# Row maxima of the attention scores in two waves per step, with jobs placed anew and the values behind them

## The reference

```python
# L0: attention over 1024 positions with 32 latent channels, then a second one over 128 concepts
th, ph, g = conv1x1(x, w_theta), conv1x1(x, w_phi), conv1x1(x, w_g)
sa_out = gamma_sa * conv1x1(softmax(th^T ph) applied to g, w_o) + x
out = gamma_moca * conv1x1(attention(conv1x1(sa_out, w_theta), concepts), w_o) + sa_out
# L1: class scores, norms, a small gate network; prob * gate is projected back and added to x
# L2: per image: group norm (32 groups), qkv, 8 heads of 32 channels, attention over 1024 positions
weight = softmax((q * scale)^T (k * scale));  h = w_proj @ (weight @ v) + b_proj;  x = x + h
# L3: group norm, qkv, attention of the 8 heads of one position among each other, projection, + x
```

## Time and profile before

| | |
|---|---|
| median of 3 runs | 1922.93 us (1922.35 to 1927.69) |
| the profiled execution | 1920.26 us, span 1918.5 us |
| busy share PE / DVE / ACT / POOL | 89% / 72% / 41% / 71% |
| L0's two windows with the work of L0 and L1 between | 53.5 to 235 us |
| rest of L0 and L1, first image prepared | 235 to 369 us |
| sixteen windows of L2 | 369.4 to 1469 us |
| L3 | 1469 to 1918.5 us |

### The profile page before, as it was taken

How to read it: one execution, slowest core, us unless ns; L and a number is a source line. 1 busy time by engine, 2 the same in 40 slices (tenths; PEclk the granted TensorE clock), 3 DMA queues, 4 the chain that set the end, 5 groups by cost and what they waited for, 6 DMA issues and landing times.

```text
span 1918.5 us, 37187 instructions
## 1 busy us (share of the span) xinstructions
PE 1702.5 (89%) x15160; PEld 773.6 (40%) x15160; DVE 1374.5 (72%) x2153; ACT 787.1 (41%) x1546; POOL 1357.7 (71%) x581
## 2 busy tenths in 40 slices
PE   5897765799999999999999999999997678889974
PEld 2332222344344444344344344444442345555541
DVE  5677567887777877767867877777771158878875
ACT  0352401155455555455455455455555233333320
POOL 0573600088788887887888878878789059989996
PEclk8898887799999999999999999999998889999986
DMA  5000030220001001001001010010010211222211
GB/s 189 1 2 1 2 129 0 84 77 23 2 2 67 2 2 67 2 9 60 2 24 45 2 59 11 1 67 2 2 45 1 89 29 55 88 77 75 74 51 47
DMA packets 48432, 75.11 MB, mean 39 GB/s; under 512 B 30804, under 2 KB 31110, under 8 KB 48262
## 3 DMA queue, kind: packets, MB, share of 16 engines
q1 hardware_dynamic: 38758, 72.15, 10.6%
q10 hardware_dynamic: 9504, 0.59, 0.3%
HBM read 44.87 MB, written 25.17 MB: 37 GB/s over the span
## 4 chain that ended last, share of the span: by engine, by line
PE 77%; DVE 13%; issue 3%; ACT 2%; DMA 2%; POOL 1%; SPq 1%; POOLq 0%; DVEq 0%; ACTq 0%
PE AV L652 14%; DVE MX L1292 7%; PE S L626 6%; PE RB L895 6%; PE S L688 4%; PE S L603 3%; PE AV L908 3%; PE RB L626 3%; PE RB L944 3%; PE S L638 2%; PE RB L603 2%; PE S L630 2%; PE S L678 2%; PE RB L688 2%; PE S L634 2%
## 5 line engine op out<-in xcount | busy, mean ns | idle before, releaser
L1201 POOL TENSOR_TENSOR ACC<-ACC,PR 128x1024 f32<-128x1024 f32 x360 | 840.9, 2373 | 34.4 <-ACT PR L1034 34.4
L1034 ACT ACTIVATE PR<-S 128x512 f32<-128x512 f32 x667 | 358.6, 603 | 373.1 <-PE S L638 242.9
L1292 DVE TENSOR_REDUCE MX<-S 128x1 f32<-128x512 f32 x646 | 409.4, 681 | 124.2 <-PE RB L603 60.5
L1201 POOL TENSOR_TENSOR ACC<-PR 128x1024 f32<-128x1024 f32 x72 | 168.9, 2368 | 343.0 <-ACT PR L1034 131.6
L652 PE MATMUL AV<-PR,VT 128*32 128x512 f32 x2304 | 312.9, 616 | 3.8 <-ACT PR L1034 3.3
L1292 DVE TENSOR_REDUCE MX<-RB 128x1 f32<-128x512 f32 x336 | 218.5, 681 | 73.8 <-PE S L603 57.0
L1034 ACT ACTIVATE PR<-RB 128x512 f32<-128x512 f32 x328 | 183.7, 604 | 168.9 <-PE S L638 63.4
L626 PE MATMUL S<-HI 32*128 32x512 f32 x667 | 195.6, 493 | 6.2 <-DVE NMR L1305 2.5
L1227 POOL TENSOR_TENSOR PR<-WO,WRK 128x1792 f32<-128x1792 f32 x32 | 155.6, 4883 | 27.9 <-DMA WO<-WO 12.9
L1227 POOL TENSOR_TENSOR PR<-WO,VT 128x1792 f32<-128x1792 f32 x32 | 155.0, 4867 | 10.3 <-DMA WO<-WO 8.3
L603 PE MATMUL S<-HI 32*128 32x512 f32 x646 | 156.2, 507 | 3.4 <-ACT PR L1034 2.8
(11 more groups left out here) (357 smaller groups left out, 3250.9 us busy)
## 6 DMA issues: line engine op xcount, KB each, us to landing
X<-out_y SPq DMA_DIRECT2D x24, 1024.0 KB, 5.0
out_y<-X SPq DMA_DIRECT2D x16, 1024.0 KB, 4.9
X<-in_x SPq DMA_DIRECT2D x8, 1024.0 KB, 8.5
OHU<-out_y SPq DMA_DIRECT2D x8, 512.0 KB, 4.4
X<-out_y SPq DMA_DIRECT2D x8, 512.0 KB, 4.1
out_y<-X SPq DMA_DIRECT2D x8, 512.0 KB, 3.1
out_y<-OHU SPq DMA_DIRECT2D x8, 512.0 KB, 3.1
WO<-WO SPq DMA_DIRECT2D x128, 16.0 KB, 1.9
```

The costliest lines, as they stand in the source:

```text
L1034: nc.scalar.activation(exps(s, pair)[:, HALF * one:HALF * one + HALF], RING[ring.place()], ACT.Exp, scale=1.0 if i is None else float(D) * ...
L1201: nc.gpsimd.tensor_tensor(ACC[:, pair, :], so_far, exps(s, pair), ALU.add).then_inc(pool_used, 1)
L1292: nc.vector.tensor_reduce(out=MX[:, h, t, keys:keys + 1], in_=bank(), op=ALU.max, axis=AX.X).then_inc(ring_free, 1)
```

## The change

1. **Waves.** A tile of maxima (four heads) becomes two waves of two heads, and the keys' first half is done for all tiles before the second. Each of the eight steps of a half carries two waves: `max` is the first job of the step and `late` the last.
2. **Order on PE.** Values no longer follow the scores: the order is scores, first wave, job, second wave, values. Where a step has no job with a bank, the second wave goes behind the values. The last step of each half does the values of the step before and its own, then the flip; the first step of a half has no values.
3. **Banks.** `Ring.begin` lays down the banks of a step ahead, in the order in which they are expected to come free, in place of strict turns.
4. **Jobs** move: q/k products from steps 1, 2, 3 and 11 (or 15) to 2, 4, 10 and 11 (or 12); value products are two of four key tiles (were four of two), at 0 or 3 and at 8; `post` from 4, 6, 12, 15 to 3, 5, 12, 15; statistics, `gn` up to two steps later. `QK_ORDER` is k, q, k, q.
5. **Waits.** `scores` waits for the flip only before its last round. The semaphore `stage_ready` goes; PE waits for the count of drained banks instead. ACT copies `AV` (`keep_values`) ahead of the exponents of the first step of a half.

```diff
     def begin(self, jobs, single):
+        held = []
+        def take():
+            if not self.free:
+                self.free.append(held.pop(0))
+            self.step.append(self.free.pop(0))
+            return self.step[-1]
+        for _ in range(H):
+            held.append(take())
+        for job in jobs:
+            for n in range(places(job, single)):
+                slot = take()
+                held.insert(2 * n + 1 if job[0] == "max" else len(held), slot)
+        self.free += held
...
-QK_ORDER = ((1, 0), (1, 1), (0, 0), (0, 1))
+QK_ORDER = ((1, 0), (0, 0), (1, 1), (0, 1))
...
-            for n, tile in enumerate(maxima(1 - half)):
-                jobs[first + (n if n <= SUM_AT else n - 1)].append(tile)
-            jobs[first + MT - 1] += [("negate", 1 - half), ("flip", 1 - half)]
+            waves = maxima(1 - half)
+            for step in range(first, first + MT):
+                jobs[step].append(waves.pop(0))
+                late[step] = [("late",) + waves.pop(0)[1:]]
+            jobs[step] += late[step] + [("negate", 1 - half)]
+            late[step] = [("flip", 1 - half)]
...
-        for step, job in zip((1, 2, 3, MT + (3 if post or gn or single else 7)), QK_ORDER):
+        for step, job in zip((1, 2, 3, MT + 3) if single else (2, 4, MT + 2, MT + (3 if gn else 4)), QK_ORDER):
-        parts = (6, MT + 1) if single else (7, MT + 1, MT + 1, MT + 2) if gn else (4, 6, 7, MT + 2)
+        for n, step in enumerate((6, MT + 1) if single else (0 if gn else 3, MT)):
...
-        for step, job in zip((4, 6, MT + 4, MT + 7), ((0, 0), (1, 0), (0, 1), (1, 1))):
+        for step, job in zip((3, 5, MT + 4, MT + 7), ((0, 0), (1, 0), (0, 1), (1, 1))):
...
-        jobs[first + 1].append(("stats", 1, ahead))
-        jobs[first + 2].append(("gn", 0, ahead))
+        jobs[first + (2 if ahead == 2 else 1)].append(("stats", 1, ahead))
+        jobs[first + (4 if ahead == 2 else 3)].append(("gn", 0, ahead))
...
@@ window of PE @@
+                    ring.begin(jobs[s], i is None)
                     scores(u, par, s)
-                    if s:
-                        values(u, par, s - 1)
-                    for job in jobs[s]:
+                    last = s % MT == MT - 1
+                    idle = all(places(job, i is None) == 0 or job[0] in ("max", "late") for job in jobs[s])
+                    behind = [job for job in jobs[s] if job[0] == "flip" or job[0] == "late" and idle and not last]
+                    for job in jobs[s][:len(jobs[s]) - len(behind)] + [("values",)] + behind:
+                        if job[0] == "values":
+                            if s % MT:
+                                values(u, par, s - 1)
+                            if last:
+                                values(u, par, s)
```

More of the change, by code:

```diff
@@ L137, in window_jobs @@
         jobs[first].append(("stats", 0, ahead))
-        jobs[first + 1].append(("stats", 1, ahead))
-        jobs[first + 2].append(("gn", 0, ahead))
+        jobs[first + (2 if ahead == 2 else 1)].append(("stats", 1, ahead))
+        jobs[first + (4 if ahead == 2 else 3)].append(("gn", 0, ahead))
     if gn:
-        jobs[MT + 4].append(("gn", 1, 1))
-    return jobs
+        jobs[MT + 5].append(("gn", 1, 1))
+    for step, stage in side:
+        jobs[step].append(stage)
+    return [job + waves for job, waves in zip(jobs, late)]
 AFTER = [("reread", 0), ("encode", 0), ("concepts", 0), ("softmax", 0), ("encode", 1), ("turn", 0), ("mix", 0),
@@ L154 @@
 AFTER_AT = (3, 3, 4, 5, 5, 6, 7, 7, 8, 9, 10, 10, 11, 12, 13, 13, 14, 15)
-START = [("v", 0)] + maxima(0)[:4] + [("v", 1)] + maxima(0)[4:] + [("negate", 0), ("flip", 0), ("weights",)]
+START = [("v", 0)] + maxima(0)[:8] + [("v", 1)] + maxima(0)[8:] + [("negate", 0), ("flip", 0), ("weights",)]
 def after_jobs():
-    jobs = window_jobs(nxt=False)
+    jobs = window_jobs(nxt=False, side=[(3, ("spread", -1))] + list(zip(AFTER_AT, AFTER)))
     jobs[SPREAD_AT].remove(("spread", -1))
-    jobs[3].append(("spread", -1))
-    for step, stage in zip(AFTER_AT, AFTER):
-        jobs[step].append(stage)
     return jobs
@@ L587, in qk_l0 @@
                 last.then_inc(ring_full, 1)
+            def qk_l0(g, which, half):
+                placed_l0(g, which, half)
+                kept_qk[g, which, half] = drained.now()
             def v_l0(g, part):
-                qk_l0(g, 2, part)
+                placed_l0(g, 2, part)
                 all_read()
@@ L596, in v_l0, with max_scores @@
                 last.then_inc(ring_full, 1)
-            def max_scores(u, par, half, t, keys):
-                if t == 0 and keys == 0:
-                    wait(pe, stage_ready, 2 * u + half + 1)
+            def max_scores(u, par, half, n):
+                keys, t, pair = n // (2 * TILES_HALF), n // 2 % TILES_HALF, n % 2
+                if n % (2 * TILES_HALF) == 0:
+                    wait(pe, ring_free, max(kept_qk[u, 0, half], kept_qk[u, 1, keys]))
                 first = HALF * half + P * t
-                for h in range(H):
+                for h in (2 * pair, 2 * pair + 1):
                     mm(bank(), HI[par][D * h:D * h + D, 0, first:first + P],
@@ L674, in v_product @@
                     pe.wait_ge(wv_in, 16)
[L675 to L676 removed]
+                for m in range(4):
+                    mt = 4 * part + m
                     for t in range(CT):
@@ L690, in qk_product @@
                 last.then_inc(ring_full, 1)
+                kept_qk[u, which, half] = drained.now()
             def group_sums(k, batch):
@@ L1020, in window @@
                 for s in range(STEPS):
+                    ring.begin(jobs[s], i is None)
+                    if s == 0 and ("sums",) in jobs[SUM_AT]:
+                        keep_values(u - 1, 1 - par, 1)
+                    if s == MT:
+                        keep_values(u, par, 0)
                     for h in range(H):
@@ L1270, in split_qk, with keep_v @@
                                                op1=ALU.subtract).then_inc(ring_free, 1)
[L1271 to L1278, removed]
+            def keep_v(u, par, part, bias):
+                src, n = bank(), 4
+                wait(dve, av_done, STEPS * (u - 1))
                 nc.vector.tensor_tensor(VT[par][:, n * part:n * part + n, :],
```

94 lines of the change are left out of this document (46 added, 48 removed).

## The result

The changed kernel takes 1934.87 us (median of 5 runs, 1933.24 to 1936.72) beside 1922.93 us before: ratio 1.0071, 95% interval 1.0053 to 1.0089. It is 11.9 us slower, and the interval excludes no change. 1918 us and "no change" were forecast; the time is inside the range (1892 to 1943), but the kernel became slower where the sum had it 5 us faster.

What follows compares the result with a forecast made beforehand. PE was taken to set the time, with waits for banks and DVE. Window terms summed to about -5 us; with 2.7 us from profiled execution to median, 1920.3 - 5 + 2.7 = 1918 us, 8-in-10 range 1892 to 1943.

Steps and rivals of the forecast that it cites:

- The price of a wave: Job steps: a second wave adds one PE round, 0.23 us (bounds 0 and 0.43), so q/k steps go from 4.48 to 4.71.
- Jobless steps and half ends: Jobless steps cost 2.4 to 2.5 us of PE work, 2.9 in a row; half ends wait slightly longer, 0.15 us exposed at flip.
- steps 0 and 1 together 8.1: Par 0 window (A), start of a half: scores with flip 1.0, wave 0.55, values product 2.0, then 4.65 less overlap.
- the +3.4 of the sum: L2 windows: seven of par 0 (A) +8.4 us, seven of par 1 (B) -5 us.
- rival 1: Job steps: second wave waits for a bank and holds values up; slower, 1946 us, milder 1932; chance 0.24.
- I keep it: Par 1 windows (B): the half-clock stretch, 1.5 us in about every second one, was said to be kept in the forecast.
- 17.6 now: Par 1 windows (B), steps 11 to 14 with statistics: 17.4 us forecast against 17.6 in the kernel before.
- stays DVE's work: Statistics steps: DVE order wave, 1.7 us statistics, wave; the chain of reductions and statistics stays on DVE, 17.4 us in B.
- Rival 2: Banks were the main loss: B windows gain 4 to 5 us, 1890 us; faster, in full or part, 0.36.
- rival 3: Clock: new waits at half ends add one half-clock stretch in each window, 15 x 1.5 = 22 us, 1940 us; chance 0.08.
- the first window: First window, 73.3 us before: -1 us, half of the gain eaten by second waves at half clock.
- Last window -3.5: Last window, jobless steps: four steps at 0.5 us and step 1, together -3.5 us.

Runs made afterwards that it cites:

- e5: Changed kernel with values in front and both maxima waves together before the job, in job steps except a half's first and last, banks there in turn: 1897.97 us.
- e1: Changed kernel with the sums job put in front of both maxima waves in steps 1 and 9: 1921.34 us.
- e2: Changed kernel with the statistics on DVE behind the second wave of their step instead of between the two waves: 1921.67 us.
- e10: e9 with the statistics last on DVE in their steps: 1885.58 us.
- e9: e5 with the two waves kept apart in steps 6, 14 and the `gn` step: 1900.66 us.
- e4: Changed kernel with the wait for the flip before all four score rounds of a half, not the last only: 1970.41 us.
- e11: e9 with one values job a step, a half's last values back in the next half's first step: 1945.15 us.
- e3: Changed kernel with the seven banks taken strictly in turn, as in the kernel before: 1939.03 us.

## Why the prediction was wrong

**The price of a wave: right.** 4.71 us was forecast for a q/k step, 4.70 measured; e5 takes the second wave out of these steps and they fall to 4.50. The round costs 0.2 us. The Trainium skill ("TensorE: Matmul & The Clock Gate", "Back-to-back issue gap") gives 216 ns between two matmuls of 512 columns in isolation and 131 ns in a sustained stream; the 0.20 us measured here, for a round of matmuls side by side, lies by the first.

**Jobless steps and half ends: right.** 2.4 and 2.7 us (2.4 and 2.9 forecast), step 7 4.6 us (4.5), A's step 15 6.3 (6.2), B's steps 0 and 1 7.4 (7.6), B's 11 to 14 17.1 undisturbed (17.4).

**The step that failed: "steps 0 and 1 together 8.1".** In A they took 9.2 us, and steps 8 and 9, for which 8.1 was taken too, 9.1 in A and in B. I had looked for banks that the second wave waits for, and not for those that the *next* step waits for when no values lie between. These three places at 1.0 us are 21 us over seven pairs; without them the A and B windows would have come out at +6 us, near the +3.4 of the sum, and the kernel 8 us of span faster instead of 13 slower. The trace shows the wait and its releaser, and e1, which moves the sums between, brings the steps down to 4.6 us. It is rival 1's mechanism (a wave needs a bank that DVE reads), but behind a step without values, not in the job steps where rival 1 had it.

**The clock: left out of the sum, and undersized.** The prediction says of the half-clock stretch of B "I keep it", but its -0.7 us sets a sum without any stretch (68.4) against a mean of the kernel before that holds them (69.0). Kept, the sum is 69.1 and B's term about +1 us in place of -5. In the same way "17.6 now" for B's steps 11 to 14 holds such a stretch; without one they take 16.1 us before, so the forecast 17.4 was 1.3 us longer, not 0.2 shorter. Measured, B windows average 1.2 us above the undisturbed 68.7, before 0.9 above 68.1. Over seven windows the 1.2 is 8 us. It and the 21 us above are more than the 24 us by which A and B windows missed; the other steps came out about 6 us below the forecast. e2 removes the gaps in front and these stretches with them. That order on DVE was forecast to be no matter ("stays DVE's work"); e2 and e10 show that it is worth 1.0 and 0.6 us of an undisturbed B window, and about 2 with the clock.

**The other rivals.** Rival 2 (banks were the main loss, B below 66 us) didn't occur. Nor did rival 3 in its form: the granted clock in A windows stayed at 1.00, and the time at half clock in the first fifteen L2 windows rose from 17 to 20 us only.

**Errors that helped:** the first window gained 5.6 us, not 1; 4.3 of it lie in step 1, which lost four maxima and their DVE time (10.5 to 6.3 us). "Last window -3.5" came out as -4.3 by luck. The window itself grew by 0.5 us: its jobless steps gained 0.7 us each, and its step 9 lost 4.5 (9.0 us, before 4.6), 3.3 of it a wait for POOL. The gain lies in L3, "untouched" in the prediction and 4.7 us shorter, with 73 us at half clock where the kernel before has 83. That this is the whole of it was not tested. Before and after:

```profile
1469.00:1918.40 449.40, 350.46 (x4831) 198.28 (x4830) 297.65 (x354) 135.01 (x311) 335.04 (x99) 0.91 0.19 62
1486.70:1931.40 444.70, 348.88 (x4834) 197.91 (x4830) 296.99 (x353) 135.25 (x311) 332.56 (x99) 0.92 0.19 63
```

**Where the gain of the change went.** The waits that it aimed at did go: the time from the first head's scores to the last head's, summed over the 32 steps of an undisturbed pair, fell from 13.4 to 3.4 us (part of this only moved, since in B's step 12 the first wave now waits for the statistics). The pair is 3.6 us longer even so. Of the 10 us some 4.6 (23 x 0.2) went into rounds in job steps, which by e5 and e9 buy something only in steps 6, 14 and the `gn` step, and 2.7 into the waits of steps 1 and 9. The remaining 6 us were not traced to single steps. By e4 and e11 the change needs its late flip wait and its double values: without the one the changed kernel is 35 us slower, without the other e9 is 44.

## What to carry over

When results go through a small ring of banks, price each reordering twice: for the instruction that is moved, and for the one behind it that now arrives sooner at a bank not yet read. Splitting a batch to get banks back early pays only where the next user wants them at once; elsewhere it is a round more on the busy engine. Put work that no one waits for (here the statistics on DVE) behind work that frees a bank. And when windows come with and without a stretch at half clock, compare like with like, in a forecast too: a clean sum set beside a mean that holds such stretches looks like a gain.

## What was not expected of the hardware

Stretches at half clock (the 1.2 GHz level) came with small gaps of PE, and unevenly. In the first fifteen L2 windows they make 3 us in e10, 17 in the kernel before, 20 in the changed one, 24 in e9, 44 in e4 and e11, but only 10 in e3, whose gaps are hardly smaller than the changed kernel's. A stretch of 3.4 us costs some 1.5 us (B windows of the kernel before: 68.1 without one, 69.6 or 69.7 with). So an edit that opened 0.65 us a half end cost 35 us where its own waits make 22 to 24. An edit can also look dead for this reason: e9's A windows won 11 us over e5 and its B windows lost 12, of which the clock makes some 9.
